# Scores times values as 64x64 squares of the array, with another order of work at the start and between the token halves, in a linear-attention decoder layer

## The chip, the cores and the metric

The kernel runs on one core of one Trainium2 chip. The metric is the device time in microseconds (us), median of 3 runs. Engines are named as in the profile: PE is TensorE (PEld its weight loads), DVE VectorE, ACT ScalarE, POOL GpSimd, SP SyncE, which issues the transfers.

## The reference

A decoder layer over 2048 tokens (32 sequences of 64), width 512. The change touches only its first part, a decayed linear attention of 32 heads of 128:

```python
x = x + attn(layernorm(x))        # then a cross attention and a product with eye, not touched
def attn(h):
    q, k, v = silu(h @ qkv_w.T)                    # 32 heads, head size 128
    scores = (q @ k.T) * decay                     # causal, inside a sequence of 64
    y = scores @ v
    y = y * rsqrt(mean(y*y over all 4096) + eps)
    return (sigmoid(h @ gate_w.T) * norm_w * y) @ out_w.T
```

A sequence attends only within its 64 tokens, so in a tile of 128 tokens (two sequences) the scores are two 64x64 blocks on a diagonal.

## The kernel before

**Tiling.** The 2048 tokens are two halves of 1024; each half is 8 token tiles of 128. The heads are taken in 8 quads of 4. One pass of `body(half, d)` (there are 16) is a unit: one half and one quad. Every fp32 factor is cut into a high and a low part in a faster 32-bit format, and a product is three products of parts (high-high, low-high, high-low), 512 columns each in `project` (L790, L793, L795), 256 in `project_v` (L808, L811, L813). The projections use a seven-product scheme of the Strassen kind (`PRODUCTS`) over 2x2 blocks: POOL makes the four sums of a weight (`mix`, L304 to L309, four instructions), and the sums of the normalised tokens (`token_sums`, L295 to L300).

**A unit on PE**, in order: VA and VB (values, 84 products each), QK0, `make_scores`, QK1, `make_scores`, G01 (gates), `weigh` of s=0 for b=0 and b=1, QK2, the first four output tiles (`project_out`, 6 products each), `make_scores`, QK3, four more output tiles, `make_scores`, G23, `weigh` of s=1 for b=0 and b=1. The eight output tiles of s=1 are put into the next unit, two each behind VA, VB, QK0 and QK1. In every seven-product call the third product waits for ACT to have copied the first out of its bank (`ready_for`, n == 2, L776; `snapshot`, L431).

**`make_scores`** (L817) has 16 products, two by two on the column halves of the array (128 rows, 64 columns, 64 moving columns). **`weigh`** (L827) has 8 products for two heads and four token tiles: the stationary block is 128x128 of v, the moving one a 128x128 tile of `scores`, whose off-diagonal blocks POOL set to zero once (L344). Full fp32 products are two records each in the trace. A call writes head h to bank `y_bank[b][h]`.

**The chain behind `weigh`:** ACT squares each head's bank (`square`, L486, into `sq[:, h]`, which POOL adds up, L335; for b=1 ACT waits until POOL has added the same buffer), DVE multiplies by the gate in place (`gated`, L630), ACT cuts the high part (`y_high`, L493), DVE the low (`y_low`, L635), then ACT squares b=1, and only then comes ACT's snapshot for the next projection (L434).

**Output tiles** go to banks 0, 1, 7, 0, 0, 1, 5, 6 in s=0 and 0, 1, 0, 1, 0, 1, 5, 6 in s=1 (`out_bank`, L182); DVE adds each to `attn_acc` (`add_out`, L649), and in s=0 it also cuts weights between these additions (L712). Bank 7 is the one of `make_scores` too, hence PE's wait at L930.

**Start.** SP loads ident, tokens of tile 0, the two weights VA and VB, tiles 1 to 3. DVE makes mean and variance (L656, L659), POOL the inverse root (L285, L287), DVE the normalised tokens (`normalise`, L666, into the idle `qk` and `v`), POOL the token sums, PE transposes (`turn`, 14 transposes a tile, L856), ACT and DVE cut them (L498, L673). PE turns tiles 0 to 2 ahead of VA, tile 3 behind it.

**Change of halves.** In the last unit of half 0, DVE takes all the statistics of half 1 behind QK3 (L720); POOL makes all token sums behind its work for the unit (L361 to L366); PE turns tile 0 behind the last `weigh`, then multiplies output tiles 0 and 1, then turns tiles 1 to 3; VA of half 1 waits for all of them (L889).

```python
for h in range(HG):                       # weigh, L827
    for i in range(TT):
        k = nc.tensor.matmul(bank[:, y_bank[b][h], r], v[:, b, i, ...128 columns], scores[:, h, b * TT + i], ...)
    k.then_inc(pv_mm, 1)
```

## Time and profile before

| | |
|---|---|
| median of 3 runs | 2196.38 us (2195.99 to 2198.97) |
| the profiled execution's own time | 2197.48 us |
| its span | 2195.6 us |
| PE busy | 2114.8 us, 96% |
| DVE, ACT, POOL busy | 1450.6, 1136.8, 758.1 us (66%, 52%, 35%) |
| mean granted TensorE clock | 0.988 |
| HBM read, written | 104.09 MB, 4.19 MB |

The span is 1.9 us short of the execution's time, and the execution lies 1.1 us over the median. Busy time of PE is modelled, since products overlap; the distance between the starts of two products says what one costs. PEclk is the granted clock in tenths of full speed.

### The profile page before, as it was taken

The page shows a single profiled execution, that of the slowest core. Times are in us where ns is not written, and L with a number is a line of the kernel's source. Part 1 is how long each engine was busy: PE and PEld are TensorE (multiplying, and loading weights), DVE is VectorE, ACT ScalarE, POOL GpSimd, SP SyncE. Part 2 cuts the span into 40 slices and gives each one's busy share as a digit, 9 for nine tenths or more (in the row PEclk, how much of TensorE's full clock was granted, in tenths as well). Part 3 has the DMA queues.
Part 4 walks back from the last instruction along what each step waited for, and adds up shares of the span by engine and source line. Part 5 has one row for each costly group of instructions (what it writes and reads, how often), then busy time and mean ns, then how long its engine had stood idle before and what let it go on. Part 6 is the DMA issues. An engine that isn't in the chain of part 4 may idle for free. (4 is left out here: it accounts for less than half of the span.)

```text
span 2195.6 us, 37208 instructions
## 1 busy us (share of the span) xinstructions
PE 2114.8 (96%) x13392; PEld 1752.8 (80%) x13392; DVE 1450.6 (66%) x2053; ACT 1136.8 (52%) x1927; POOL 758.1 (35%) x883
## 2 busy tenths in 40 slices
PE   4999999999999999989999999999999999699998
PEld 4788888888888888878888888888888888466665
DVE  5566657666666666766666666667666665588885
ACT  3554545454545555545454554545454554466664
POOL 6342425252434343343334342425252432111110
PEclk9999999999999999989999999999999999899999
DMA  2211111111212021111111111111111111301110
GB/s 89 79 50 50 49 49 49 49 49 38 60 32 66 29 65 34 46 35 40 60 40 56 42 49 49 49 49 49 47 51 38 60 31 50 127 30 44 49 44 20
DMA packets 40495, 109.37 MB, mean 50 GB/s; under 512 B 4960, under 2 KB 9568, under 8 KB 40288
## 3 DMA queue, kind: packets, MB, share of 16 engines
q1 hardware_dynamic: 40416, 108.30, 15.8%
q8 instruction: 51, 0.84, 0.2%
q14 instruction: 28, 0.23, 0.0%
HBM read 104.09 MB, written 4.19 MB: 49 GB/s over the span
## 5 line engine op out<-in xcount | busy, mean ns | idle before, releaser
L304 POOL TENSOR_TENSOR raw<-raw 128x256 f32<-128x256 f32 x128 | 100.7, 787 | 605.8 <-DMA raw<-w_pairs 605.7
L790 PE MATMUL bank<-x_hi,w_hi_c 128*128 128x512 f32 x672 | 266.1, 396 | 6.9 <-ACT gate L434 3.9
L795 PE MATMUL bank<-x_hi,w_lo_c 128*128 128x512 f32 x672 | 262.7, 391 | 0.0
L793 PE MATMUL bank<-x_lo,w_hi_c 128*128 128x512 f32 x672 | 262.3, 390 | 0.0
L840 PE MATMUL bank<-wo_hi,y_hi 128*128 128x512 f32 x512 | 202.5, 396 | 2.7 <-DVE y_lo L635 2.7
L841 PE MATMUL bank<-wo_lo,y_hi 128*128 128x512 f32 x512 | 201.9, 394 | 0.0
L842 PE MATMUL bank<-wo_hi,y_lo 128*128 128x512 f32 x512 | 201.9, 394 | 0.0
L434 ACT ACTIVATE qk<-bank 128x512 f32<-128x512 f32 x192 | 115.1, 600 | 143.6 <-PE bank L795 143.0
L335 POOL TENSOR_TENSOR sq_acc<-sq_acc,sq 128x512 f32<-128x512 f32 x124 | 160.2, 1292 | 81.9 <-ACT sq L486 68.7
L597 DVE TENSOR_TENSOR qk<-bank,qk 128x512 f32<-128x512 f32 x192 | 127.3, 689 | 85.2 <-ACT qk L457 42.6
L790 PE MATMUL bank<-x_hi,w_hi_a 128*128 128x512 f32 x448 | 177.9, 397 | 0.0
L649 DVE TENSOR_TENSOR attn_acc<-attn_acc,bank 128x512 f32<-128x512 f32 x240 | 162.5, 683 | 19.5 <-PE bank L842 18.4
L795 PE MATMUL bank<-x_hi,w_lo_a 128*128 128x512 f32 x448 | 174.8, 390 | 0.0
L793 PE MATMUL bank<-x_lo,w_hi_a 128*128 128x512 f32 x448 | 174.6, 390 | 0.0
L324 POOL TENSOR_TENSOR qk<-qk,sq 128x512 f32<-128x512 f32 x64 | 82.7, 1292 | 219.7 <-ACT sq L455 219.7
L790 PEld LDWEIGHTS bank<-x_hi,w_hi_c 128*128 128x128 f32 x672 | 126.5, 188 | 34.9 <-ACT gate L434 4.4
L795 PEld LDWEIGHTS bank<-x_hi,w_lo_c 128*128 128x128 f32 x672 | 126.5, 188 | 26.9
L590 DVE TENSOR_TENSOR bank<-bank,qk 128x512 f32<-128x512 f32 x128 | 89.6, 700 | 87.8 <-PE bank L795 87.0
L793 PEld LDWEIGHTS bank<-x_lo,w_hi_c 128*128 128x128 f32 x672 | 126.7, 188 | 25.1
L630 DVE TENSOR_TENSOR bank<-bank,gate 128x512 f32<-128x512 f32 x128 | 88.7, 697 | 79.9 <-ACT sq L486 78.1
L808 PE MATMUL bank<-w_hi_a,x_hi 128*128 128x256 f32 x448 | 130.1, 290 | 7.2 <-DVE x_lo L673 4.2
L590 DVE TENSOR_TENSOR gate<-bank,gate 128x512 f32<-128x512 f32 x96 | 66.4, 692 | 105.5 <-PE bank L795 105.5
(150 smaller groups left out, 5593.9 us busy)
## 6 DMA issues: line engine op xcount, KB each, us to landing
raw<-w_pairs SPq DMA_DIRECT2D x128, 512.0 KB, 3.5
raw<-w_out SPq DMA_DIRECT2D x32, 512.0 KB, 3.5
raw<-ctx_in SPq DMA_DIRECT2D x16, 256.0 KB, 2.9
raw<-ctx_in SPq DMA_DIRECT2D x32, 128.0 KB, 3.1
xr<-x SPq DMA_DIRECT2D x4, 1024.0 KB, 10.8
out<-attn_acc SPq DMA_DIRECT2D x16, 256.0 KB, 2.0
attn_acc<-x SPq DMA_DIRECT2D x8, 256.0 KB, 6.4
decays<-decay SPq DMA_DIRECT2D x32, 64.0 KB, 3.0
```

Source lines behind the costliest of these rows:

```text
L335: nc.gpsimd.tensor_tensor(acc, acc, sq[:, h], ALU.add).then_inc(sq_added, 1)
L434: nc.scalar.activation(dst, shaped(call, bank[:, (CHAIN, CHAIN, THIRD)[nth]]), ACT.Copy).then_inc(snapped, 1)
L590: nc.vector.tensor_tensor(dst, shaped(call, bank[:, (SECOND, CHAIN, THIRD)[nth]]), src, ALU.add).then_inc(c_added, 1)
L597: nc.vector.tensor_tensor(o, shaped(call, bank[:, at_bank]), o, ALU.mult).then_inc(silu_ready, 1)
L649: nc.vector.tensor_tensor(acc, acc, bank[:, out_bank(half, d, s, i)], ALU.add)\
L790: nc.tensor.matmul(bank[:, to], w_hi[w][:, a, s], x_hi[:, b, c], start=part in ("first", "only") and c == 0, stop=False, skip_group_check= ...
L793: nc.tensor.matmul(bank[:, to], w_hi[w][:, a, s], x_lo[:, b, c], start=False, stop=False, skip_group_check=True)
L795: i = nc.tensor.matmul(bank[:, to], w_lo[w][:, a, s], x_hi[:, b, c], start=False, stop=part in ("last", "only") and c == 1, skip_group_che ...
L808: nc.tensor.matmul(dst, x_hi[:, b, c, s], w_hi[c][:, a], start=part in ("first", "only") and c == 0 and j == 0, stop=False, skip_group_che ...
L840: nc.tensor.matmul(dst, y_hi[:, h, r], wo_hi[:, h], start=(h == 0), stop=False)
L841: nc.tensor.matmul(dst, y_hi[:, h, r], wo_lo[:, h], start=False, stop=False)
L842: k = nc.tensor.matmul(dst, y_lo[:, h, r], wo_hi[:, h], start=False, stop=(h == HG - 1))
```

## The change

It does five things.

1. `weigh` takes the four (64 keys) x (64 channels) squares of the array one by one: per head and token tile two sequences (`top`) times two channel halves (`c`), each a product with 64 rows, 64 columns and 64 moving columns. The first of a call (h = i = 0) is 128 channels wide. That is 30 products a call where there were 8. Sequence `top` goes to bank `y_bank[b][top]`, so a bank holds two heads of one sequence, and ACT and DVE read and write token halves (`by_tokens`, `y_part`). `pv_mm` rises twice, both times at the end of the call. `decay_scores` is one instruction of 128 partitions where there were two of 64; nothing is cleared any more.
2. `sq` has a buffer for each b.
3. Output tiles use banks 0, 1, 0, 1, 0, 1, 5, 6 always; tile i waits for the addition of tile i-2, and `make_scores` waits for none.
4. At the start the two weights are loaded by ACT's queue, which also loads its sigmoid table; POOL mixes them ahead of the token sums; tiles 0 and 1 are turned ahead of VA, tiles 2 and 3 within it (at its products 2, 4 and 6). The normalised tokens stay in `attn_acc`, the sums go to `sq_acc`, a spare and `qk`.
5. In the last unit of half 0 DVE takes two statistics behind each of VA, VB, QK0 and QK1 and normalises one tile in each of G01, QK2, ahead of G23 and behind it; POOL makes the token sums between its other work; output tiles 0 and 1 stand behind turned tiles 0 and 1; VA of half 1 turns tiles 2 and 3 within it, and output tiles 2 and 3 stand behind VA and VB.

```diff
-        sq = sb(own, "sq", [P, HG, BT])
+        sq = sb(own, "sq", [P, 2, HG, BT])
...
+        WITH_VALUES = whole(2)[:3], whole(2)[3:] + whole(3)[:2], whole(3)[2:]
...
-        def out_bank(half, d, s, i):
-
-            if s == 0:
-                return (0, 1, 7, 0, 0, 1, 5, 6)[i]
+        def out_bank(i):
+
             return (0, 1, 0, 1, 0, 1, 5, 6)[i]
...
@@ sync
-                    if p == 0:
-                        load(raw1, w_pairs[0, VA], raw1_landed)
-                        load(raw0, w_pairs[0, VB], raw0_landed)
@@ gpsimd
                 def squares(half, d, s):
                     for b in range(2):
+                        pool.wait_ge(sq_made, count(half, d, 8, 4 * s + 2 * b + 2))
                         for h in range(HG):
...
+                    if half == 0 and at(d, LAST):
+                        inv_roots(slice(0, HT), 2 * HT, TT + 1)
                     mix1(half, d, 2, 4)
...
                     last_block(half, d, QK2)
+                    if half == 0 and at(d, LAST):
+                        token_sums(1, 0)
                     if following:
                         mix1(half, d, 3, 5)
                         mix0(half, d, 5)
+                    if half == 0 and at(d, LAST):
+                        token_sums(1, 1)
                     last_block(half, d, QK3)
+                    if half == 0 and at(d, LAST):
+                        token_sums(1, 2)
                     if following:
                         mix0(half, d, 6)
+                    if half == 0 and at(d, LAST):
+                        token_sums(1, 3)
                     squares(half, d, 1)
...
+                mix1(0, 0, 0, 1)
+                inv_roots(slice(0, HT, TT), 2, 1)
+                mix0(0, 0, 0)
+                inv_roots(slice(1, HT, TT), 4, 2)
+                token_sums(0, 0)
+                token_sums(0, 1)
+                inv_roots(slice(2, HT, TT), 6, 3)
+                token_sums(0, 2)
+                inv_roots(slice(3, HT, TT), 8, 4)
+                token_sums(0, 3)
@@ scalar
                 def square(half, d, s, b):
+                    if s or before(half, d):
+                        act.wait_ge(sq_added, count(half, d, 8, 4 * s + 2 * b - 2))
+                    for top in range(2):
+                        act.wait_ge(pv_mm, count(half, d, 8, 4 * s + 2 * b + top + 1))
+                        nc.scalar.activation(by_tokens(sq[:, b], top), y_part(b, top), ACT.Square).then_inc(sq_made, 1)
...
+                    if at(d, 0):
+                        project(half, d, VA, *(lambda i=i: turned_hi(half, WITH_VALUES[i]) for i in range(3)))
+                        for part in range(2):
+                            cut_qk0(half, d, part)
@@ vector
+                    if before_turning:
+                        normalise(1, 1)
                     cut_a(half, d, 2, 1)
                     for i in range(2):
                         add_out(half, d, 0, i)
...
+                turned_lo(0, whole(0, 1))
+                normalise(0, 2)
+                statistics(0, (3, 3 + TT), 6)
                 normalise(0, 3)
@@ tensor
                     for n, (a, b, to, part) in enumerate(PRODUCTS):
+                        if call == VA and at(d, 0) and n in (2, 4, 6):
+                            turn(half, WITH_VALUES[n // 2 - 1])
                         ready_for(half, d, call, n)
...
                 def weigh(half, d, s, b):
                     for h in range(HG):
                         for i in range(TT):
-                            r = slice(i * P, (i + 1) * P)
-                            k = nc.tensor.matmul(bank[:, y_bank[b][h], r],
-                                                 v[:, b, i, (s * HG + h) * HD:(s * HG + h + 1) * HD],
-                                                 scores[:, h, b * TT + i], start=True, stop=True)
-                        k.then_inc(pv_mm, 1)
+                            first = (s * HG + h) * HD
+                            wide = HD if h == i == 0 else SEQ
+                            for top in range(2):
+                                keys, to = slice(top * SEQ, (top + 1) * SEQ), (h * TT + i) * SEQ
+                                for c in range(0, HD, wide):
+                                    k = nc.tensor.matmul(bank[c:c + wide, y_bank[b][top], to:to + SEQ],
+                                                         v[keys, b, i, first + c:first + c + wide],
+                                                         scores[keys, h, b * TT + i], start=True, stop=True)
+                                if h == HG - 1 and i == TT - 1:
+                                    k.then_inc(pv_mm, 1)
...
-                        if i == 2 and s == 1:
-                            pe.wait_ge(out_added, count(half, d, 16, 9))
-                        if i == 3:
-                            pe.wait_ge(out_added, count(half, d, 16, 8 * s + (1, 2)[s]))
                         if i == TT:
                             pe.wait_ge(y_ready, count(half, d, 8, 4 * s + 4))
-                            pe.wait_ge(out_added, count(half, d, 16, 8 * s + (4, 3)[s]))
-                        if i == TT + 1:
-                            pe.wait_ge(out_added, count(half, d, 16, 8 * s + 4))
+                        if 2 <= i < 6:
+                            pe.wait_ge(out_added, count(half, d, 16, 8 * s + i - 1))
...
-                    pe.wait_ge(out_added, count(half, d, 16, 3))
                     make_scores(half, d, 1, 0)
...
-                        turn(1, 0)
-                        rest_out(half, d, 1, (0, 1))
-                        turn(1, 1)
-                        turn(1, 2)
-                        turn(1, 3)
+                        turn(1, whole(0))
+                        rest_out(half, d, 1, (0,))
+                        turn(1, whole(1))
+                        rest_out(half, d, 1, (1,))
```

## Rows read from the trace of the kernel before

**Rows 1.** The page: busy time, share of the span and instructions.

```profile
PE 2114.8 (96%) x13392; PEld 1752.8 (80%) x13392; DVE 1450.6 (66%) x2053; ACT 1136.8 (52%) x1927; POOL 758.1 (35%) x883
```

**Rows 2.** Groups by line and form, as the page: busy us, mean ns, idle before.

```profile
L831 PE MATMUL bank<-scores,v 128*128 128x128 f32 x1024 | 119.5, 275 | 0.0
```

**Rows 3.** PE in order of time at a `weigh` pair (start, duration, line, operation).

```profile
327.04 0.40 PE L795 MATMUL bank<-x_hi,w_lo_b 128*128 128x512 f32 x1
327.27 3.74 PE L831 MATMUL bank<-scores,v 128*128 128x128 f32 x32
330.76 0.48 PE L790 MATMUL bank<-x_hi,w_hi_c 128*128 128x512 f32 x1
331.08 0.40 PE L793 MATMUL bank<-x_lo,w_hi_c 128*128 128x512 f32 x1
```

**Rows 4.** PE in order of time at a `make_scores`.

```profile
250.13 0.40 PE L842 MATMUL bank<-wo_hi,y_lo 128*128 128x512 f32 x1
250.46 1.15 PE L823 MATMUL bank<-qk 128*64 128x64 f32 x32
251.54 0.50 PE L790 MATMUL bank<-x_hi,w_hi_c 128*128 128x512 f32 x1
251.88 0.39 PE L793 MATMUL bank<-x_lo,w_hi_c 128*128 128x512 f32 x1
```

**Rows 5.** PE in order of time, cross attention: four products on four squares.

```profile
1946.60 0.64 PE L1265 MATMUL bank<-raw,wq 64*64 64x512 f32 x1
...
1946.62 0.64 PE L1266 MATMUL bank<-raw,wk 64*64 64x512 f32 x1
1947.08 0.59 PE L1265 MATMUL bank<-raw,wq 64*64 64x512 f32 x1
```

**Rows 6.** ACT, DVE and PE in order of time around two `weigh` pairs.

```profile
328.50 0.60 ACT L486 ACTIVATE sq<-bank 128x512 f32<-128x512 f32 x1 [0.43 <-PE bank L831]
...
332.17 0.60 ACT L486 ACTIVATE sq<-bank 128x512 f32<-128x512 f32 x1 [0.46 <-POOL sq_acc L335]
332.66 0.59 ACT L434 ACTIVATE qk<-bank 128x512 f32<-128x512 f32 x1
...
329.22 1.37 DVE L630 TENSOR_TENSOR bank<-bank,gate 128x512 f32<-128x512 f32 x2 [2.33 <-ACT sq L486]
...
374.03 3.74 PE L831 MATMUL bank<-scores,v 128*128 128x128 f32 x32
...
379.25 0.60 ACT L434 ACTIVATE v<-bank 128x512 f32<-128x512 f32 x1
```

**Rows 7.** DVE and PE in order of time, output tiles of s=0.

```profile
344.49 0.68 DVE L649 TENSOR_TENSOR attn_acc<-attn_acc,bank 128x512 f32<-128x512 f32 x1
...
346.86 0.34 PE L823 MATMUL bank<-qk 128*64 128x64 f32 x4 [0.71 <-DVE attn_acc L649]
```

**Rows 8.** Stretches (us): busy time of each engine, PEclk, DMA share, GB/s.

```profile
390.46:400.53 10.07, 10.07 (x85) 10.07 (x84) 3.67 (x6) 3.44 (x6) 1.07 (x1) 1.00 0.17 52
928.30:943.80 15.50, 11.57 (x45) 9.06 (x44) 11.82 (x18) 4.80 (x8) 4.99 (x6) 0.89 0.35 107
943.80:965.90 22.10, 16.56 (x102) 13.07 (x100) 18.32 (x31) 12.25 (x23) 19.00 (x24) 0.86 0.01 2
965.90:992.30 26.40, 24.92 (x180) 24.20 (x181) 11.72 (x17) 10.97 (x18) 4.63 (x6) 0.92 0.07 20
32.80:54.10 21.30, 15.45 (x100) 15.01 (x98) 10.79 (x17) 9.24 (x16) 11.50 (x14) 0.84 0.20 61
54.10:67.40 13.30, 11.81 (x84) 11.61 (x84) 4.17 (x6) 4.22 (x7) 2.79 (x4) 0.87 0.52 183
```

**Rows 9.** POOL in order of time at the start.

```profile
26.25 0.73 POOL L300 TENSOR_TENSOR v<-v 128x256 f32<-128x256 f32 x1
...
31.12 1.32 POOL L300 TENSOR_TENSOR qk<-qk 128x256 f32<-128x256 f32 x1
```

**Rows 10.** Groups by line and form again: the first inverse roots.

```profile
L285 POOL TENSOR_SCALAR rstd<-mv 128x2 f32<-128x2 f32 x4 | 1.1, 280 | 8.9 <-DVE mv L659 8.9
```

More of the change, by code:

```diff
@@ L292, in token_sums @@
                     n = (half * TT + p) * 4
-                    b11, b21, b12, b22, t1, t2, t3, t4n = (staged(p, slice(i * 256, (i + 1) * 256)) for i in range(8))
+                    b11, b21, b12, b22 = normed(half, p)
+                    t1, t2, t3, t4n = summed(p)
                     pool.wait_ge(xn_ready, (half * TT + p) * 2 + 2)
+                    if half == 1 and p >= 2:
+                        pool.wait_ge(s_mm, count(0, LAST, 4, 4))
                     nc.gpsimd.tensor_tensor(t1, b12, b11, ALU.subtract).then_inc(t_made, 1)
@@ L477, in square @@
                 def square(half, d, s, b):
-                    for h in range(HG):
-                        act.wait_ge(pv_mm, count(half, d, 8, 4 * s + b * HG + h + 1))
-                        if b == 0:
-                            act.wait_ge(c22_ready, count(half, d, 6, (4, 6)[s]))
-                            if s or before(half, d):
-                                act.wait_ge(sq_added, count(half, d, 8, 4 * s + h - 1))
-                        else:
-                            act.wait_ge(sq_added, count(half, d, 8, 4 * s + h + 1))
-                        nc.scalar.activation(sq[:, h], bank[:, y_bank[b][h]], ACT.Square).then_inc(sq_made, 1)
@@ L488, in y_high @@
-                def y_high(half, d, s, b):
-                    for h in range(HG):
-                        act.wait_ge(y_made, count(half, d, 8, 4 * s + b * HG + h + 1))
-                        if b == 1:
-                            act.wait_ge(out_mm, count(half, d, 16, 8 * s + TT))
-                        nc.scalar.activation(y_hi[:, h], bank[:, y_bank[b][h]], ACT.Copy).then_inc(y_hi_ready, 1)
-                def turned_hi(half, p):
-                    for r in range(4):
+                    if b == 0:
+                        act.wait_ge(c22_ready, count(half, d, 6, (4, 6)[s]))
@@ L717, in body @@
                     project(half, d, QK3)
-                    if half == 0 and at(d, LAST):
-                        dve.wait_ge(x_rest_landed, 16)
-                        statistics(1, range(HT), HT)
                     for i in range(TT):
@@ L843, in project_out, with turn @@
                     k.then_inc(out_mm, 1)
-                def turn(half, p):
-                    n = half * TT + p
-                    for r in range(4):
+                def turn(half, pieces):
+                    for p, r in pieces:
+                        n = half * TT + p
                         if r == 0:
```

252 lines of the change are left out of this document (134 added, 118 removed).

## The prediction, made blind

> **What bounds the kernel.** I read the page first: PE is busy for 96% of the span and no other engine for more than 66% [rows 1]. Then PE in order of time, where a unit repeats every 112.8 us almost without a gap; so PE's own pitches count, and any chain that PE would catch up with once it is faster. Then the stages by windows, for the start and the change of halves, where PE does idle [rows 8]. The profiled execution took 2197.5 us (span 2195.6 and 1.9 around it), 1.1 over the median of 2196.4; I take my savings off the median. A measurement of this kernel tells about 0.2%, or 4.4 us, from no change.
>
> **weigh, on PE.** Before: 1024 records, busy for 119.5 us [rows 2]. A pair of calls (there are 32) runs its 32 records in 3.49 us, 0.11 each; from the start of the last product before it to the start of the second product behind it are 331.08 - 327.04 = 4.04 us [rows 3].
>
> After: 60 products, 120 records. How fast do squares go? `make_scores` shows two tiles at once: 32 records whose starts spread over 1.15 - 0.22 = 0.93 us, that is 15 steps of 0.062 us with two records in each [rows 4] (0.22 is the median length of one record in that group). Four squares at once are shown in the cross attention alone: the four high records start within 0.02 us, their low ones 0.48 us later, where 512 columns at two cycles each need 0.43 at 2.4 GHz [rows 5]. That is one burst of eight records, but neither four squares nor the shared rows slowed it. I take four a round.
>
> What speaks against the change is the cost of changing the array's shape. Into `make_scores` the start-to-start distance is 0.33 us where the usual one is 0.23; behind its last round 0.15 us pass (1.08 - 0.93), and the next product takes 0.34 to its successor, 0.11 too much [rows 4]. The trace thus puts about 0.1 us on the way in and 0.2 on the way out. A call of `weigh` now has two shapes, 64x128 for its first two products and 64x64 for 28. So a pair of calls has five changes of shape instead of none. A call: the wide step 0.11 [rows 3], its first load uncovered 0.05, leaving it 0.15, then 14 rounds: 13 x 0.062 + 0.15 = 0.96; together 1.27 us, a pair 2.53. With the way in and out: 0.33 + 2.53 + 0.34 = 3.20 against 4.04. PE gains 0.84 a pair, 27 us over 32 pairs.
>
> **weigh, the chain behind it.** The third product of the next projection waits for ACT's snapshot, which stands behind squares, gates and high parts. Before, with 0 at the first `weigh` record: first square at 1.23 (328.50 - 327.27), snapshot at 5.39 to 5.98 [rows 6]; PE's third product at 331.08 + 11 x 0.228 - 327.27 = 6.31. So ACT was only 0.3 us early. After, the first square can't start when a head is done but at the end of the call: 1.27 - 0.15 + 0.22, and the 0.1 that a hand-over takes: 1.43. The chain from there was 4.16 us, of which 0.46 was ACT waiting for POOL [rows 6]; the second buffer of `sq` takes that away: 3.70. Snapshot 5.13 to 5.73, third product at 5.8. PE alone would be there at 2.53 + 0.34 + 11 x 0.228 = 5.38: a new stall of 0.4 us. Saved in s=0: 6.31 - 5.8 - 0.1 (way in) = 0.41. In s=1, with 0 at 374.03, VA follows; its products are 0.12 us apart (10.07 / 84, the first one 0.09 longer), so its third step was at 3.49 + 24 x 0.12 + 0.09 = 6.46, the snapshot ending at 5.8 [rows 6, 8]; after 5.9 with the way in: 0.56. Together 0.97 a unit, 15.5 us in 16 units. The longer strides of ACT and DVE I cost at nothing, since rows of equal element count differ by under 2% (0.59 and 0.60; 1.37 for two and 0.68) [rows 6, 7].
>
> **Output tiles of s=0.** PE waited 0.71 us before `make_scores` for the addition out of bank 7 [rows 7]. After, tile 3 waits for DVE's second addition instead, which ends at 344.49 + 0.68 = 345.17; six products of 0.23 and the way in bring `make_scores` to 346.7 instead of 346.86. Nearly all of that wait comes back as one in front of tile 3: 0.15 a unit, 2.4 us. The halved `decay_scores`, the clearing and the loads of ACT's queue lie beside PE's work: nothing.
>
> **Start.** Before, VA starts at 32.8 us, behind POOL's sums of tile 2; a tile costs POOL (31.12 + 1.32) - (26.25 + 0.73) = 5.5 us [rows 9]. After, VA waits for two tiles: 27.3. POOL also idled 8.9 us for DVE's means [rows 10] and now mixes a weight in that time; weights now share the transfers with tile 0, so I give it half: 22.9. VA itself: 10.07 us [rows 8], 28 transposes at 0.11, and about 4.6 of waiting for POOL's tiles 2 and 3, which come 5 us apart: 17.8, where the stretch to VB was 21.3 with the clock at 0.84 [rows 8]. VB starts at 40.7 instead of 54.1: 13.4 us. The 13.3 us behind (clock 0.87, waits for silu) I leave. Bounds 8 and 18: POOL late, or VB at full clock.
>
> **Change of halves.** G23 of the last unit took 15.5 us [rows 8] where 42 products of 0.228 make 9.7: 5.8 us lost behind the lump of statistics, all of it spread now. From `weigh` to QK0 were 22.1 + 26.4 = 48.5 us [rows 8]. After: ACT's chain ends 5.1 us in, four high copies to 7.1, DVE's low ones to 8.1, an addition, four more low ones: VA at 11.0; then 10.07 + 3.1 for transposes + 1.6 for the last silu, an output tile 1.4, VB 10.07, a tile 1.4: 38.6. That is 9.9 saved. Given back in that unit: normalising tile 1 stands ahead of the cut that DVE's additions wait behind (1.5 us, the wait of tile 2), and some 1 us from POOL's sums ahead of weights. Net 13.2; bounds 6 and 17.
>
> **Sum.** 15.5 + 2.4 + 13.4 + 13.2 = 44.5; 2196.4 - 44.5 = 2152 us. With the bounds of each part (chain 12 to 22) 2138 to 2168.
>
> **Rivals.**
> - *The chain or the shapes take all of the weigh gain* (a strided read slower, a change of shape 0.3 us): 2196.4 - 29 = 2167. For: ACT's margin was 0.3 us. Against: each instruction has the same size. 0.15.
> - *Order gains nothing much*: POOL is the queue at the start, and its sums now stand ahead of weights in the last unit; start and turn together bring 8: 2196.4 - 18 - 8 = 2170. 0.10.
> - *Records are issued no faster than two a round.* The longest run of small products in the trace never beats two per 0.062 us [rows 4]; the four-fold burst had been waiting for a semaphore, ready to go [rows 5]. Then a call is 0.31 + 27 x 0.062 + 0.15 = 2.13, a pair with its ends 4.93: 0.89 slower than now, 28 us in all, against 29 gained: 2196. 0.10. The Trainium skill ("TensorEngine Tiling (Array Packing)", Instruction Overhead) has a related rule, about 60 cycles for each matmul however short; taken per record it would be 0.025 us at 2.4 GHz, 120 of them 3.0 us a pair, and no gain worth the name. The burst [rows 5] doesn't bear it out.
> - *Slower: squares that share 64 rows or a bank go one after another.* Place: every `weigh`. One record a round: 56 x 0.062 + 0.7 = 4.2 a call, a pair 9.0 with its ends, 5 more than now: 160 - 29 = 131 us slower, 2327. It decides from a pair of calls over 4.4 us, 37 ns a record. Against: four squares in 0.02 us [rows 5]. 0.05.
>
> **The numbers.** Forecast 0.60 with 2138 to 2168 as its own range; the two partial cases fill 2160 to 2180. The range 2133 to 2180 leaves out the last two rivals and some tails. Faster by over 0.2%: 0.60 + 0.25 + a fifth of the third rival, 0.87; within: 0.07; slower: 0.06.
>
> **What would show it.** In the profile after: a pair's first to last record in about 2.4 us with four starts inside 0.03 us; a wait "PE <- ACT snapshot" of some 0.4 us behind G01; `make_scores` no longer waiting for an addition, but `project_out` doing so; VA's first product near 23 us, VB near 41, G23 of the last unit in 10 us. Starts in twos, or a gap of more than 0.2 us between the wide and the narrow products, would make it wrong; so would PE idle behind POOL in the last unit of half 0.

## The result: 2189.7 us, faster by 0.3% where 2% was forecast, and the profile after

| | before | after |
|---|---|---|
| median | 2197.15 us (20 runs, 2195.81 to 2198.97) | 2189.72 us (20 runs, 2187.14 to 2196.04) |
| ratio | | 0.9969, 95% interval 0.9962 to 0.9975 |
| span of the profiled execution | 2195.6 us | 2188.1 us |
| mean granted TensorE clock | 0.988 | 0.985 |

The forecast was 2152 us, with a range of 2133 to 2180. The time lies 10 us above the range. Of the 44.5 us that were to be saved, 7.4 were.

The page of the kernel after, its engines, the groups of `weigh` (L877), and one row that had no counterpart before, the instruction fetches (queue 8); it answers to [rows 1, 2]:

```profile
PE 2104.3 (96%) x16208; PEld 1712.8 (78%) x16208; DVE 1398.7 (64%) x1989; ACT 1128.1 (52%) x1927; POOL 748.6 (34%) x882
...
q8 instruction: 105, 1.72, 0.3%
...
L877 PE MATMUL bank<-scores,v 64*64 64x64 f32 x3584 | 66.9, 222 | 0.0
...
L877 PE MATMUL bank<-scores,v 64*128 64x64 f32 x256 | 28.1, 296 | 0.0
```

The same row of the page before:

```profile
q8 instruction: 51, 0.84, 0.2%
```

PE in order of time and ACT beside it, kernel after, around the `weigh` pair of s=0 (start, duration); it answers to [rows 3, 6]:

```profile
312.52 0.39 PE L835 MATMUL bank<-x_hi,w_lo_b 128*128 128x512 f32 x1
...
312.83 2.76 PE L877 MATMUL bank<-scores,v 64*128 64x64 f32 x120
...
314.28 1.09 ACT L518 ACTIVATE sq<-bank 128x512 f32<-128x512 f32 x2 [0.74 <-PE bank L877]
...
315.52 0.50 PE L830 MATMUL bank<-x_hi,w_hi_c 128*128 128x512 f32 x1
...
315.86 0.40 PE L833 MATMUL bank<-x_lo,w_hi_c 128*128 128x512 f32 x1
...
317.69 0.62 ACT L466 ACTIVATE qk<-bank 128x512 f32<-128x512 f32 x1
```

The pair takes 315.52 - 312.83 = 2.69 us where it took 3.49. That is the work the change was made of, and it came close to the forecast (2.53). Now the pair of s=1, once in half 0 and once in half 1:

```profile
358.97 2.76 PE L877 MATMUL bank<-scores,v 64*128 64x64 f32 x120
...
362.16 0.38 PE L850 MATMUL bank<-w_hi_a,x_hi 128*128 128x256 f32 x1 [0.44 <-issue]
...
1274.04 2.76 PE L877 MATMUL bank<-scores,v 64*128 64x64 f32 x120
1280.07 0.38 PE L850 MATMUL bank<-w_hi_a,x_hi 128*128 128x256 f32 x1 [3.27 <-issue]
...
1282.82 0.37 PE L853 MATMUL bank<-w_lo_b,x_hi 128*128 128x256 f32 x1 [0.93 <-issue]
```

Here the loop over the quads jumps back. In half 0 the next product comes 3.19 us after the pair's start, in half 1 6.03 us, and "issue" says that PE waited for no engine and no transfer of data. Stretches of the kernel after (us; busy time of PE, PEld, DVE, ACT, POOL; PEclk, DMA share, GB/s), first one unit of half 0 and one of half 1, then those that answer to [rows 8]:

```profile
359.00:471.00 112.00, 111.37 (x887) 93.74 (x886) 70.10 (x98) 57.57 (x93) 42.91 (x46) 1.00 0.15 48
1274.00:1392.50 118.50, 114.11 (x887) 96.34 (x886) 70.00 (x98) 57.79 (x93) 41.87 (x46) 0.97 0.15 47
26.20:40.70 14.50, 13.36 (x111) 12.98 (x112) 9.66 (x19) 6.82 (x13) 11.15 (x16) 1.00 0.01 1
40.70:54.50 13.80, 10.65 (x87) 10.27 (x86) 8.50 (x12) 6.88 (x12) 5.18 (x8) 1.00 0.59 189
912.50:922.30 9.80, 9.80 (x47) 7.81 (x43) 7.50 (x12) 4.81 (x8) 6.49 (x8) 1.00 0.41 135
922.30:961.40 39.10, 36.35 (x369) 32.87 (x368) 25.48 (x42) 21.64 (x41) 14.93 (x18) 1.00 0.05 15
```

The start (VB at 40.7 us, QK0 at 54.5 where it was 67.4) and the change of halves (9.8 + 39.1 = 48.9 us where it took 15.5 + 48.5 = 64.0) came close to the forecast (40.7 us, and 9.7 + 38.6 = 48.3). The units tell the rest. The distance from one `weigh` pair of s=1 to the next, taken from the trace, in us:

```
unit           1      2      3 to 6         7      8      9      10     11     12     13     14
before         112.9  112.8  112.8          118.4  132.1  113.0  112.9  112.9  112.8  112.9  112.9
after          111.7  112.1  112.0          115.3  122.4  111.8  117.6  118.5  117.5  116.8  118.4
```

Five units of half 1, exactly those entered by a jump back to a loop that half 0 runs at 112.0, take 117 to 118.5. They cost 28.5 us more than five units of half 0. Beside them stands the extra traffic: the transfers of a unit of half 1 (page section 3, cut to 1274.0:1392.5) hold

```profile
q8 instruction: 9, 0.15, 0.5%
```

while the same section for 359.0:471.0 has no such row. Before, no pass of either loop behind its first fetched instructions.

The loss stands at the start of the pass. In the five passes PE is 4.8 to 6.4 us behind a pass of half 0 when it is through with VA, and no further behind at the end of the pass. What the wait was for is told by the packets of the instruction queue: in the pass shown, the first two behind the pair run from 1277.14 to 1278.05 and from 1280.18 to 1281.21, and in all five passes VA's first product starts 1.95 to 2.05 us after the end of the first packet.

PE's part of the loop had grown from 1480 instructions to 1833 (700 products where there were 612; a full fp32 product is four instructions, load and product twice, and a split one two; 65 others).

### The profile page after: what moved, and what is told of

The parts are those of the page before. It is cut to its first block and busy times, and to the rows that moved or that the text cites. A ratio compares the mean times of both kernels' runs of the same rounds, so it can differ in the third digit from the quotient of the medians.

```text
span 2188.1 us, 42500 instructions
## 1 busy us (share of the span) xinstructions
PE 2104.3 (96%) x16208; PEld 1712.8 (78%) x16208; DVE 1398.7 (64%) x1989; ACT 1128.1 (52%) x1927; POOL 748.6 (34%) x882
## 3 DMA queue, kind: packets, MB, share of 16 engines
q1 hardware_dynamic: 40128, 107.25, 15.5%
## 5 line engine op out<-in xcount | busy, mean ns | idle before, releaser
L329 POOL TENSOR_TENSOR raw<-raw 128x256 f32<-128x256 f32 x128 | 113.3, 885 | 578.0 <-DMA raw<-w_pairs 577.9
L887 PE MATMUL bank<-wo_hi,y_hi 128*128 128x512 f32 x512 | 207.3, 405 | 9.1 <-DVE y_lo L670 3.0
L665 DVE TENSOR_TENSOR bank<-bank,gate 128x512 f32<-128x512 f32 x128 | 82.7, 692 | 80.7 <-ACT sq L518 80.7
```

Source lines behind the costliest of these rows:

```text
L887: nc.tensor.matmul(dst, y_hi[:, h, r], wo_hi[:, h], start=(h == 0), stop=False)
```

## Experiments

**Theory A:** PE keeps a loop loaded if it fits; the longer body happens not to stay loaded in half 1, so it is fetched again in every pass. **Theory B:** half 1 is slow for something else that the change brought (engines' chains after the new change of halves, traffic, clock).

### 63 more instructions ahead of everything

```diff
+                for _ in range(128):
                     pe.wait_ge(const_landed, 16)
                 turn(0, whole(0, 1))
```

> The kernel after, with 63 more instructions (waits that are long satisfied) on PE ahead of its first transposition, where PE waits for x anyway; nothing else. Theory A (PE's loop body, 1833 instructions or 7.2 blocks of 16 KB, stays loaded where it touches eight blocks and is fetched again in every pass where it touches nine; half 1's loop happens to touch nine): shifted by 63 both loops touch eight, the 9 fetches a unit disappear from half 1's loop, a unit there takes 112 us as in half 0 instead of 118, six units give 34 to 38 us: 2152 to 2157 us. Theory B (the second half is slower for something else: the DVE and POOL chain after the turn, DMA traffic, the clock): no change, 2190 us.

(Two of these waits make one instruction: 128 of them are 64, where there was one.)

Measured: 2161.15 us (4 runs), ratio to before 0.984 (0.9824 to 0.9857). The kernel is 28.6 us faster for 63 more instructions that do nothing. The unit of half 1, and the end of a pass:

```profile
1269.10:1381.20 112.10, 111.48 (x887) 93.78 (x886) 70.20 (x98) 57.73 (x93) 42.97 (x46) 1.00 0.15 48
```

```profile
1269.13 2.76 PE L877 MATMUL bank<-scores,v 64*128 64x64 f32 x120
1272.31 0.38 PE L850 MATMUL bank<-w_hi_a,x_hi 128*128 128x256 f32 x1 [0.42 <-issue]
```

The whole page counts 59 instruction fetches instead of 105, and none in a pass behind a loop's first. Theory B falls, since no other engine's work changed. The time stays 4 us above what theory A gave: I had counted six slow units, and only the five that a jump back enters are slow (28.6 us in all, 5.7 each).

### 15 more, and 64 more ahead of half 1's loop alone

The first has 32 in the place of 128 in the edit above. The second:

```diff
                     body(half, 0)
+                    for _ in range(128 if half == 1 else 0):
+                        pe.wait_ge(const_landed, 16)
                     with nc.Fori(1, LAST, engines=[pe.engine], hint_back_edge=True) as d:
```

> The same with 15 more instructions instead of 63. Theory A: the two loops begin 5637 instructions apart, which is 22 blocks and 5 instructions, so half 0's loop stands only just inside eight blocks; 15 more push it over too, and both loops are fetched anew in each pass: half 0's unit goes from 112 to 118 us, 2190 + 35 = 2220 to 2230 us. Theory B: 2190 us.

> The kernel after with 64 waits that are long satisfied on PE just ahead of half 1's loop, so that half 0's loop stays where it was. Theory A: as with 63 at the start, 2152 to 2160 us (64 waits at a place where PE works cost up to 2 us once). Theory B: 2190 to 2192 us.

Measured: 2161.94 and 2171.19 us (one run each), 59 fetches in both. The first is a miss: both loops stayed loaded. So the bad places are fewer, or elsewhere, than I had them. In the second the fetches went too, but the unit in which the waits stand took 120.5 us instead of 111.8. The distance from the pair to VA grew by 7.1 us, so 64 waits that were long satisfied cost 0.11 us each; the other 1.6 us fall in VA, of which a part ran at a granted clock of 0.50. I had put 2 us in all. Half 0 was untouched, so it was half 1's loop, and the place of that loop alone, that cost the time.

### The order without the squares

The kernel after with the 128x128 products and all that belongs to them (scores with zero blocks, one `sq`, counts by head), a body of 1481:

```diff
-                            wide = HD if h == i == 0 else SEQ
...
+                            k = nc.tensor.matmul(bank[:, y_bank[b][h], r],
+                                                 v[:, b, i, (s * HG + h) * HD:(s * HG + h + 1) * HD],
+                                                 scores[:, h, b * TT + i], start=True, stop=True)
+                        k.then_inc(pv_mm, 1)
```

> The kernel after with the 128x128 products of before in weigh (block scores with zeros, squares, gates and sums by head, one square buffer), and with the new order at the start, at the change of halves and for the output tiles. Its loop body is 1480 instructions again, 5.8 blocks, inside eight wherever it starts. Theory A: what the traces show of the order is kept, 12.9 us at the start, 15.2 at the change, and up to 2.4 of output tiles: 2197 - 28 = 2166 to 2170 us, faster than the whole change. If the second half is slow because of the new order (theory B): 2197 - 28 + 34 = about 2200 us.

Measured: 2176.82 us (4 runs), ratio 0.9912 (0.9895 to 0.9928). The order alone is worth 20 us, more than the whole change, which theory B can't give; its units in the loops take 112.8 as before. It is 8 us less than I expected. Most of that is the change of halves: the two units around it take 241.4 us instead of 250.5, a gain of 9.1 where I had 15.2, because I had read the gain from G23 to QK0 alone and in the kernel after. From `weigh` to QK0 it is 41.3 us here instead of 39.1, and the unit ahead gives back: behind QK2 the four output tiles take 8.3 us instead of 6.2, and the products around them 1.5 us more.

### Tall products: two at a time instead of four

```diff
-                            wide = HD if h == i == 0 else SEQ
+                            wide = HD
```

> The kernel after with every product of weigh on 64x128 weights (one for each sequence, head and row) instead of two 64x64 squares, so two run at a time instead of four; banks, layout and everything else as they are. Loop body 1609 instructions, 6.3 blocks. If what counts on PE is array cells used per product, two at a time take as long as four half as wide: a pair of calls 64 records at 2 x 21.3 ns, 2.7 us as now; and with the body short enough the fetches in half 1's loop go: 2160 us, like the 63 more instructions. If squares run faster than tall products (each record as long as a square's, but only two at a time, is the same 2.7; records issued one at a time would be twice that, 5.1 us a pair), 32 pairs x 2.6 = 2160 + 83 = 2240 us.

Measured: 2184.37 us (4 runs), ratio 0.9941 (0.9924 to 0.9958). The body of 1609 instructions is fetched in no pass behind the first. A pair:

```profile
1284.12 3.79 PE L877 MATMUL bank<-scores,v 64*128 64x64 f32 x64
1287.83 0.39 PE L850 MATMUL bank<-w_hi_a,x_hi 128*128 128x256 f32 x1
```

It takes 3.71 us, between the two values expected: half as many records as the squares have, on average 2.6 times as long each (3.71 / 64 = 0.058 against 2.69 / 120 = 0.022, with the changes of shape). The starts of the records show why. In the kernel after, four squares start within 0.02 us and the next four 0.058 us later; here two tall products start within 0.01 us and the next two 0.112 us later, which is the step of one 128x128 product with twice the columns (0.11). So a round of two tall products takes nearly twice as long as a round of four squares; what holds it up isn't shown. The squares carry the whole gain of `weigh`: with tall products it is 0.22 us slower a pair than before. There is also no wait behind the jump here: 64 records last longer than 120 short ones. Neither price I gave was right, and the short body alone doesn't make the better kernel.

### The jump moved away from the short products

```diff
-                def body(half, d):
+                def values_of(half, d):       # VA, VB and their output tiles
...
+                def heads_of(half, d):        # QK0 and all behind it
...
                 for half in range(2):
-                    body(half, 0)
-                    with nc.Fori(1, LAST, engines=[pe.engine], hint_back_edge=True) as d:
-                        body(half, d)
-                    body(half, LAST)
+                    for d in range(2):
+                        values_of(half, d)
+                        if d == 0:
+                            heads_of(half, d)
+                    with nc.Fori(1, LAST - 1, engines=[pe.engine], hint_back_edge=True) as d:
+                        heads_of(half, d)
+                        values_of(half, d + 1)
+                    heads_of(half, LAST - 1)
+                    values_of(half, LAST)
+                    heads_of(half, LAST)
```

> The kernel after with PE's loop turned: its body begins with QK0's products and ends with the value products and output tiles of the next unit, so that the jump back follows 24 output products of 512 columns and not 120 short products; the order of PE's work is the same. Body 1834 instructions. Theory: the 0.50 us behind a weigh call at the jump (2.69 us where no jump follows, 3.19 where one does) is the sequencer not being far enough ahead; moved, 2.69 to 2.79 us in all 16 units: 10 passes x 0.45 + 2 x 0.25 = 5 us off. Where the loops come to stand is drawn anew: 2156 us if neither is fetched in each pass, 2185 if one is, 2213 if both. Rival (the 0.5 us belongs to the products, not to the jump): 3.19 stays.

Measured: 2156.47 us (4 runs), ratio 0.9815 (0.9798 to 0.9831), and both loops stayed loaded. The same place of the program as above, in half 1:

```profile
1265.19 2.76 PE L877 MATMUL bank<-scores,v 64*128 64x64 f32 x120
1267.92 0.38 PE L850 MATMUL bank<-w_hi_a,x_hi 128*128 128x256 f32 x1
```

2.73 us instead of 3.18, and nothing comes back at the new jump. So 0.45 us a pass was the jump's, seen only where the products ahead of it are too short to cover it; 4.7 us in all.

### Is it the place of the loop?

Half 1's loop was fetched again, half 0's was not, though by my count of instructions they begin 5636 apart, 22 times 256 and 4 (the count was wrong, see below). The Trainium skill ("Runtime: NRT & Kernel Launch", Instruction fetch mechanics) says that instructions come in blocks of 256 into a store that for PE holds 2048. The trace agrees with the block (each packet of the instruction queue is 16,384 bytes, 64 for each of 256), and the store is put to the test further down. I added 4, 9 and 100 at the start.

> The kernel after with 4 more waits that are long satisfied on PE ahead of all its work, so that half 0's loop comes to stand in its 16 KB block exactly where half 1's stood (place 138 of 256 by my count, the program's start not counted), and half 1's at 142. If a place in the block alone decides, half 0's loop is now fetched in each pass and half 1's may be: 2161 + 28 to 33 = 2190 or 2218 us. If it is not the place alone, half 0's loop stays loaded and the time is 2161 or 2190 us by half 1's.

> The kernel after with 9 more waits ahead of PE's work, between 4 (fetched, last fetch 6.1 us before the first jump back) and 15 (not fetched, last fetch 11.3 us before). If it is fetched, 2190 us and a last fetch about 6 us before the jump; if not, 2161 us and a last fetch some 11 us before it. Both outcomes bear out that the place of the loop decides, and they bound where; a last fetch 6 us before the jump with the loop staying loaded, or 11 with the loop fetched, speaks against the distance as the sign of it.

> The same with 100 more, places 234 and 238, where the body of 1833 touches nine blocks if the program begins on a block. If nine blocks touched is what makes the fetches, both loops are fetched in each pass: 2161 + 62 = 2220 us and a few us for the waits (64 of them cost 8.5 us where nothing hid them; here all but 2 to 5 are hidden). If not: 2163 to 2167 us.

Measured (one run each): 2190.39, 2197.48 and 2159.98 us. With 4 and 9 half 1's loop is fetched (105 fetches in all), with 100 neither. Half 0's loop stays loaded on the very place, by that count, where half 1's is fetched, and at a place where by that count nine blocks are touched. So either the place isn't what decides or my count of the place is wrong. The fetches ahead of a loop's first jump back told which. In us before that jump:

```
loop      instructions added at the start
half 0    0                    123.4 112.1 100.8 85.5 63.0 47.1 30.2 15.8
half 1    100                  123.5 111.8 100.4 85.4 60.8 47.0 36.6 15.8
half 1    0   fetched anew     115.1 109.5  95.1 73.2 57.7 45.7 27.7  6.0
half 1    9   fetched anew     115.1 109.6  95.2 73.3 57.7 46.0 27.9  6.1
half 1    15                   116.9 110.4  95.4 76.1 57.6 46.0 27.4 11.3
```

Half 1's loop with 100 more is fetched for the first time like half 0's with none, so the two don't stand 4 places apart but some 100 to 150. That gives a prediction for half 0's loop. To add so many without delaying the start I let squares of the very first unit be computed twice:

```diff
+                                again = (range(0, HD, SEQ) if half == 0 and at(d, 0)
+                                         and (i == 1 or i == 2 and s == b == 0) else ())    # 160 more
-                                for c in range(0, HD, wide):
+                                for c in (*range(0, HD, wide), *again):
```

> The kernel after with 40 squares of the very first unit computed twice (same product, same place), which puts 160 more instructions ahead of both loops and nothing inside them; about 1 us of PE time. The fetches of half 1's loop with 100 more instructions fall where those of half 0's loop fall with none (123.5, 111.8, 100.4, 85.4 us before the first jump against 123.2, 112.1, 100.8, 85.6), so half 1's loop seems to stand as half 0's would with 100 fewer, or 156 more. By that, places 156, 160 and 165 are the bad ones seen so far, and 160 more put half 0's loop on a bad one and take half 1's off it: half 0's units go to 117 to 119 us, half 1's to 112, and the total stays near 2190 us. Rival (half 1's loop alone can be fetched anew, for something that comes ahead of it): half 0's units stay at 112, and the time is 2162 us.

> The same with 16 squares of the first unit computed twice, 64 more instructions: by the same reckoning half 0's loop at 64 and half 1's at 220, both seen good: no fetches in either loop, 2162 us. It is the control for the 160 (the doubled squares by themselves cost under 1 us).

Measured: 2165.22 and 2161.09 us; neither loop was fetched again. The 160 missed, but its fetches (114.1 109.5 95.8 73.4 57.7 46.0 27.3 11.2) were those of the last line above: one step past the edge. Hence 8 and 16 fewer:

> As first_unit_160, with 38 squares of the first unit computed twice, 152 more instructions. With 160, half 0's loop stayed loaded, but its fetches before the first jump (114.1, 109.5, 95.8, 73.4, 57.7, 46.0, 27.3 us before it) were those of half 1's loop with 0 to 15 more (115.1, 109.5, 95.1, 73.2, 57.7, 45.7, 27.7) and the last one stood at 11.2 us, as that of half 1's loop with 15 more (11.3, loaded) and not as with 9 (6.1, fetched anew): it was just past the upper edge. So 152 is 8 fewer: if the place decides, half 0's loop now has its last fetch about 6 us before the first jump, is fetched in each pass, 118 us a unit, and the total is 2190 us with half 1's loop loaded. Rival (only half 1's loop can be fetched anew): 2162 to 2165 us.

> The same with 144 more, 8 further from the edge: by the place, the same as 152, 2190 us and a last fetch about 6 us before half 0's first jump. By the rival 2162 to 2165 us.

Measured: 2194.62 and 2189.35 us. Half 0's units now take 117.5 to 119.5 us (115.9 to 118.5 with 144), half 1's 112.0, and the last fetch ahead of half 0's first jump stands at 6.2 and 6.1 us. The kernel with 152, a unit of each half, then the end of a pass in half 0:

```profile
366.90:485.80 118.90, 114.07 (x887) 96.16 (x886) 69.93 (x98) 57.62 (x93) 42.06 (x46) 0.97 0.14 46
1301.70:1413.70 112.00, 111.30 (x885) 93.69 (x884) 70.12 (x98) 57.70 (x93) 43.02 (x46) 1.00 0.15 48
```

```profile
366.85 2.76 PE L878 MATMUL bank<-scores,v 64*128 64x64 f32 x120
373.13 0.38 PE L850 MATMUL bank<-w_hi_a,x_hi 128*128 128x256 f32 x1 [3.52 <-issue]
```

The stall moved from one loop to the other with not one instruction changed in either. What decides is where the loop stands. All places seen:

```
added ahead of the loop   0    4    9    15   63   64   100  144  152  160
half 0's loop             ok   ok   ok   ok   ok   ok   ok   anew anew ok
half 1's loop             anew anew anew ok   ok   ok   ok   ok   ok   ok
```

My count of the distance was wrong, and the traces show where. It took a transposition for four instructions, like a full fp32 product, but a transposition is one record in the traces where such a product is two, so it is two instructions. The 56 transpositions between the loops take off 112: the loops begin 5524 apart, 21 times 256 and 148. Both loops on one scale, place 0 where half 0's stands with none added, half 1's 148 further (of 256):

```
place           0 to 100   144    148    152    157    160    163 to 248
half 0's loop   ok         anew          anew          ok
half 1's loop   ok                anew   anew   anew          ok
```

With the right distance one stretch of places, some 14 to 59 wide, holds every bad place and no good one, for both loops.

### A body longer than the store, and a jump behind long products

64 squares a unit computed twice, as above but in every unit (i in 1 and 2), in the kernel after and in the one with the moved jump.

> The kernel after, with 64 squares a unit computed twice (the same product again on the same place, so the result is the same): PE's loop body is 2089 instructions, 8.2 blocks of 256. They take 64 x 2 x 21.3 ns = 2.7 us a unit, 44 us in all. If a body of more than 2048 can't stay loaded anywhere, both loops are fetched in each pass, and 12 passes cost 5.0 to 5.5 us each: 2161 + 44 + 60 to 66 = 2265 to 2271 us, with 8 or 9 instruction fetches a unit. If the store is larger: 2205 us and no fetches inside the loops, or one loop alone as in after: 2233.

> The same 64 doubled squares in loop_edge_moved: body 2090 instructions, the jump behind 24 output products of 512 columns. If what a fetched loop costs is the wait for the first block after the jump, it costs about as much at a place where PE has long products queued less what the queue hides: 3 to 5 us a pass, 10 passes, 2156 + 44 + 30 to 50 = 2230 to 2250 us. If the stall came only from the short products that are used up faster than the blocks come, it vanishes here though the fetches stay: 2200 us.

Measured: 2240.83 and 2195.13 us (one run each), with 161 and 155 fetches, nine or ten in each pass behind the first, of both loops in both kernels. The transfers of a unit of half 1 and the end of a pass, first `long_body`, then `long_body_edge_moved`:

```profile
q8 instruction: 10, 0.16, 0.6%
```

```profile
1318.70 0.34 PE L877 MATMUL bank<-scores,v 64*64 64x64 f32 x7 [0.72 <-issue]
1322.82 0.58 PE L850 MATMUL bank<-w_hi_a,x_hi 128*128 128x256 f32 x1 [3.77 <-issue]
```

```profile
q8 instruction: 9, 0.15, 0.5%
```

```profile
1292.44 3.79 PE L877 MATMUL bank<-scores,v 64*128 64x64 f32 x184
1296.28 0.38 PE L850 MATMUL bank<-w_hi_a,x_hi 128*128 128x256 f32 x1
```

A body of 2089 is fetched in both loops, one of 1833 only on bad places, which agrees with the 2048 that the Trainium skill states in the section named above. The same section of the Trainium skill says that a taken jump whose target is outside a window of two pages has to wait until that page is fetched, and gives no price. Two pages don't fit the runs: bodies of 1480 to 1833 instructions, over five blocks, jumped back with no fetch at all.

The doubled squares cost 1.03 us a pair, and unit 9, which no jump back enters, is 1.95 us longer in the first kernel and 1.83 in the second: 31.2 and 29.3 us in 16 units and not 44. So the fetching costs 2240.8 - 2161.2 - 31.2 = 48 us in the first and 2195.1 - 2156.5 - 29.3 = 9 us in the second. (My 12 and 10 passes counted the first pass of each loop, which no jump precedes.) The traces say where. In the first, some 44 us stand at the 10 jumps back and in VA behind them, 4.4 each; another 5.5 are waits in the middle of the squares of s=0 in half 0. In the second the new jump itself costs nothing: QK0 follows the last output product at 0.23 us in every pass, as it does with the short body, though the blocks are fetched.

```profile
1322.48 0.39 PE L889 MATMUL bank<-wo_hi,y_lo 128*128 128x512 f32 x1
1322.71 0.39 PE L830 MATMUL bank<-x_hi,w_hi_c 128*128 128x512 f32 x1
```

What is left are waits of 0.6 to 1.1 us in the squares of s=0 in half 0 (7.0 us in eight units) and up to 0.7 us a pass in half 1's VA, behind the squares of s=1. So a fetch costs nothing seen where PE has products of 512 columns ahead of it, and it costs where the short ones run out before the block is there, with a jump or without. I had expected 3 to 5 us a pass at the moved jump, which was the wrong one of the two mechanisms named.

### What the last unit of half 0 gives back

In the kernel after, DVE and PE in order of time, behind QK2 of that unit (the wait is for output tile 2):

```profile
886.52 1.79 DVE L699 TENSOR_SCALAR attn_acc<-attn_acc,mv,rstd 128x512 f32<-128x512 f32 x2
...
888.23 1.47 DVE L594 TENSOR_TENSOR w_lo_a<-raw,w_hi_a 128x768 fp32r<-128x768 f32 x1
...
889.63 0.67 DVE L684 TENSOR_TENSOR attn_acc<-attn_acc,bank 128x512 f32<-128x512 f32 x1
...
890.36 0.50 PE L887 MATMUL bank<-wo_hi,y_hi 128*128 128x512 f32 x1 [2.31 <-DVE attn_acc L684]
```

The normalisation stands ahead of the addition that frees the bank. Moved behind the scores, in the kernel with the moved jump:

```diff
                     project(half, d, QK2, lambda: cut_a(half, d, 2, 0))
-                    if before_turning:
-                        normalise(1, 1)
                     cut_a(half, d, 2, 1)
...
                     decay_scores(half, d, 1, 0)
+                    if before_turning:
+                        normalise(1, 1)
                     project(half, d, QK3)
```

> loop_edge_moved, and in the last unit of half 0 DVE normalises the second pair of half 1's tiles behind the output tiles and the scores of that unit instead of ahead of them. Nothing on PE's stream changes. Theory: the four output tiles behind QK2 of that unit take 9.89 us instead of 6.42 because each bank comes free late: DVE's two normalisations (1.86 us) and the weights' rests stand ahead of its additions. Moved, the block goes to 6.5 to 8 us and the total to 2153 to 2155 us. Rival: the wait comes from the weights' rests and from POOL, and the block stays at 9.9: 2156.5 us.

Measured: 2154.21 us (5 runs), ratio to before 0.9809 (0.9796 to 0.9822), the fastest kernel of the study. The block of four tiles takes 6.9 us (8.6 in the kernel it was made from, 9.9 in the one after), and the wait shrinks:

```profile
887.40 0.50 PE L887 MATMUL bank<-wo_hi,y_hi 128*128 128x512 f32 x1 [0.60 <-DVE attn_acc L684]
```

## Why the prediction was wrong, step by step

**The sum failed by a term that isn't in it.** It priced what PE does and not what PE is fed with: the change makes the loop's body a quarter longer in instructions (1480 to 1833), and "weigh, on PE" charged the 120 records of a pair their time on the array alone. What it takes to bring them to PE was put at nothing, without a reason. At the place where half 1's loop came to stand, this cost 28.5 us in five passes, most of the 37.7 by which the forecast missed; with the loops loaded, 2161.15 us lies inside the range. Part of it is the wait behind the jump: 6.3 us from the pair to VA on average where a loaded loop has 3.2. Part follows in VA, 12.8 us instead of 10.2: in four of the five passes a second wait, in all a lower clock. In the pass shown, right behind the first wait, the granted clock falls to 0.50, the lower of TensorE's two levels (1.2 GHz), from 1280.9 to 1287.7, and VA's products, 0.12 us apart elsewhere, are 0.21 apart until then:

```profile
1283.00:1286.00 3.00, 3.00 (x16) 3.00 (x16) 0.00 (x0) 1.54 (x2) 1.90 (x3) 0.50 0.02 5
```

Without the fetches the change gives 36 us, where I had forecast 44.5. The rest of the miss:

- **weigh on PE.** Pair 2.69 us, forecast 2.53; the mechanism (four at once, changes of shape paid on the way in and out) is right. The way in is 0.31 us from start to start and the first product behind takes 0.34 to its successor, close to the 0.33 and 0.34 of the forecast. The rounds of four are 0.058 us apart (0.062), but leaving the wide products takes 0.20 (0.15) and the first round of squares 0.11 to the next. The third rival, two a round, would have given 2.13 a call; a call takes 1.34.
- **weigh, the chain.** First square 1.45 us after the pair's start (forecast 1.43), snapshot over at 5.5 (5.73); the stall is 0.05 us, not 0.4. So s=0 saves 0.56 us, not 0.41. But s=1 saves 0.22 us, not 0.56: "In s=1 ... VA follows" overlooked that the loop jumps there, and 120 short records don't cover the jump. Together 0.78 a unit in the loops where 0.97 stood, 12.5 us instead of 15.5.
- **Output tiles.** The forecast was 0.15 a unit; the block of four tiles went from 6.46 to 6.42 us. The wait came back in front of tile 2 or 3, as I said it would, all but 0.04 of it. 0.6 us instead of 2.4.
- **Start.** VB at 40.7 us and 12.9 us gained at QK0: the forecast 40.7 and 13.4. But VA began at 26.2, not 22.9, and then ran to VB in 14.5 us, not 17.8. POOL wasn't late: its last sum for VA ended at 23.0. What the sum left out stands behind that: eight transpositions 0.21 us apart and DVE's low parts, for which VA waits. They take 3.2 us from POOL's last sum to VA, where before VA had followed the last sum by 0.4.

```profile
22.31 0.73 POOL L325 TENSOR_TENSOR spare_sums<-attn_acc,spare_sums 128x256 f32<-128x256 f32 x1
23.02 1.91 PE L909 MATMUL bank<-ident,spare_sums 128*128 128x128 f32 x8
...
26.24 0.39 PE L850 MATMUL bank<-w_hi_a,x_hi 128*128 128x256 f32 x1 [1.31 <-DVE x_lo L706]
```

The wait for tiles 2 and 3, on the other hand, was overdone: 1.4 us instead of 4.6. Two errors of 3.3 us that cancel, so that VB's 40.7 is luck.
- **Change of halves.** G23 9.8 us (forecast 9.7, though the 42 x 0.228 written there is 9.6), `weigh` to QK0 39.1 (38.6). But the unit ahead gives back more: the four tiles 3.7 us (9.9 for 6.2) and the products around them some 0.3, against the 2.5 of the forecast. Units 7 and 8 together went from 250.5 to 237.7 us, 12.8, of which 1.6 belong to `weigh`: 11.2 net, forecast 13.2.

That is 12.5 + 0.6 + 12.1 + 11.2 = 36.4 us for a kernel whose loops stay loaded, against 36.0 between the medians with 63 more instructions (12.1 is the start in that trace: the first unit's end comes 12.7 us earlier, 0.6 of it `weigh` and tiles).

**The rivals.** The measured time lies between the third (2196) and the second (2170), but none of their mechanisms is in it. All of them were about how fast the array and the engines' chains run. The chances should have held one for "PE's stream gets 24% longer, and something in feeding it doesn't scale", and the trace of before gave a hold for it: the instruction queue was idle through both loops, so a loop that no longer fits would show as a new cost.

**What stays open.** Why a place is bad. Theory A's reason, a body of 1833 that touches nine blocks of 256 on 40 of 256 places and eight on the others, would give one stretch of 40 bad places, and 2089 touches at least nine everywhere and was loaded on no place tried. The upper edge lies between 157 and 160 on the common scale. But 40 places below it would begin at about 120, and the loop of half 0 with the moved jump begins 387 instructions later (192 products of two and three others), at place 131, has 1834 instructions and was loaded. So nine blocks alone aren't shown to be the reason, and the lower edge, between 100 and 144, wasn't looked for. The last fetch at 6 us ahead of the first jump went with every bad place and none of the good ones; that it is the cause wasn't shown.

## What to carry to other kernels

Count the instructions of the loop body on the busiest engine before and after a change that splits work into smaller pieces. Where the body nears the engine's store, the time depends on where the loop stands, and a dozen instructions ahead of it can cost or give back 28 us; look at the instruction queue's packets inside the loop, per unit, before explaining anything else. Put the jump back behind long instructions, not behind short ones: it hid 0.45 us a pass here when the loop was loaded, and the whole 4.4 us a jump when it wasn't.

## What was not expected of the hardware

- A loop of 1833 PE instructions runs at 112.0 us a unit with no fetches or at 116 to 120 with nine, by its place alone; 1609 and 1480 had none behind the first pass, 2089 had nine or ten in every pass, in two kernels.
- A PE wait on a semaphore that has long passed its value costs 0.11 us where PE has no slack (64 of them, 7.1 us), and the idle time was followed by a lower clock (another 1.6 us).
- Records of 64 columns come in rounds of four every 0.058 us as 64x64 squares, and in rounds of two every 0.112 us as 64x128, no faster than one 128x128 product of 128 columns (0.11).
- 3.3 us of idle PE were followed by 6.8 us at a granted clock of 0.50, so that with a second wait the five passes lost nearly as much again in VA (12.8 us for 10.2) as at the jump (6.3 for 3.2).
